# ACT and DVE take turns in copying the 1x1 units; the third depthwise unit goes between the V transposes and the mix

## The reference

```
xn   = gn(x)
qkv  = depthwise3x3(einsum('bchw,oc->bohw', xn, w_qkv) + b_qkv) + b_dw
q, k, v in windows of 8x8, 4 heads of 16 channels      # (n, head, c, 64)
attn = softmax(einsum('nhcx,nhdx->nhcd', q, k) * temperature)
out  = einsum('nhcd,nhdx->nhcx', attn, v) * gelu(einsum('nhcx,yx->nhcy', v, w_mlp) + b_mlp)
y    = x + einsum('bchw,oc->bohw', out, w_proj) + b_proj
```

## Time and profile before

| what | us |
|---|---|
| median of 3 runs | 829.38 |
| the runs | 822.47, 829.38, 843.41 |
| profiled execution, whole | 837.38 |
| its span, first to last instruction | 835.5 |
| PE matmul busy in the span | 721.4 |
| DVE busy | 512.1 |
| ACT busy | 493.9 |

### The profile page before, as it was taken

The page is one execution under the profiler, slowest core; times in us unless marked ns, Lnnn a source line. Parts: engine busy times, 40 slices in busy tenths (PEclk is TensorE's granted clock), DMA queues, the critical chain, the costliest instruction groups (busy, mean ns, idle before and its releaser), DMA issues.

```text
span 835.5 us, 40617 instructions
## 1 busy us (share of the span) xinstructions
PE 721.4 (86%) x19080; PEld 633.8 (76%) x19080; DVE 512.1 (61%) x957; ACT 493.9 (59%) x628; POOL 0.3 (0%) x5
## 2 busy tenths in 40 slices
PE   3968988988788988988979898999899898999875
PEld 3956877887676877877867877888788777788854
DVE  2714466758666665756665574767666666656554
ACT  2553455747556465756657485767566675747564
POOL 0000000000000000000000000000000000000000
PEclk9999999999999989999999999999999999999987
DMA  9723131423416031131414140121304040412022
GB/s 224 264 100 108 18 109 54 155 84 113 149 29 210 4 131 33 58 102 30 145 18 159 18 149 15 66 98 53 110 15 150 4 159 4 157 18 104 5 65 40
DMA packets 26501, 73.69 MB, mean 88 GB/s; under 512 B 9463, under 2 KB 15991, under 8 KB 21271
## 3 DMA queue, kind: packets, MB, share of 16 engines
q1 hardware_dynamic: 26076, 69.31, 26.1%
q10 hardware_dynamic: 258, 1.79, 1.2%
HBM read 54.31 MB, written 16.78 MB: 85 GB/s over the span
## 4 chain that ended last, share of the span: by engine, by line
PE 81%; DVE 8%; issue 5%; ACT 4%; DMA 1%; DVEq 0%; ACTq 0%
PE work L596 24%; PE work L576 23%; PE pair_ps L645 9%; PE score_ps L681 9%; PE pair_ps L669 5%; PE work L547 5%; PE pair_ps L654 3%; DVE z L343 3%; DVE patches L407 3%; PE score_ps L632 3%; ACT v_t L297 2%; DMA z<-in_hot 1%; DVE stats L415 1%; DVE staged L476 0%; DVE mixed L424 0%
## 5 line engine op out<-in xcount | busy, mean ns | idle before, releaser
L576 PE MATMUL work<-consts,patches 64*100 64x192 f32 x2048 | 209.6, 345 | 27.7 <-DVE patches L407 22.7
L596 PE MATMUL work<-z,dw 109*64 109x64 f32 x6144 | 202.2, 227 | 23.9 <-issue 12.4
L596 PEld LDWEIGHTS work<-z,dw 109*64 109x64 f32 x6144 | 192.6, 142 | 29.6 <-issue 26.7
L576 PEld LDWEIGHTS work<-consts,patches 64*100 64x100 f32 x2048 | 165.0, 170 | 46.5 <-issue 33.8
L275 ACT ACTIVATE z<-work 100x768 f32<-100x768 f32 x158 | 122.2, 807 | 65.4 <-PE work L576 65.2
L275 ACT ACTIVATE qkv<-work 128x1024 f32<-128x1024 f32 x63 | 64.5, 1023 | 135.5 <-PE work L596 135.5
L343 DVE COPY z<-work 100x768 f32<-100x768 f32 x98 | 90.9, 953 | 56.4 <-PE work L576 56.3
L447 DVE TENSOR_TENSOR gate<-pair_ps,consts 128x512 f32<-128x512 f32 x64 | 44.3, 692 | 92.8 <-PE pair_ps L645 92.8
L297 ACT ACTIVATE v_t<-pair_ps 128x512 f32<-128x512 f32 x64 | 38.2, 597 | 97.9 <-PE pair_ps L654 97.9
L645 PE MATMUL pair_ps<-consts,qkv 64*64 64x64 f32 x2048 | 82.3, 233 | 11.4 <-issue 7.9
L645 PEld LDWEIGHTS pair_ps<-consts,qkv 64*64 64x64 f32 x2048 | 72.1, 145 | 23.8 <-issue 14.5
(11 more groups left out here) (45 smaller groups left out, 523.4 us busy)
## 6 DMA issues: line engine op xcount, KB each, us to landing
staged<-in_x SPq DMA_DIRECT2D x18, 1024.0 KB, 4.9
out_y<-staged SPq DMA_DIRECT2D x15, 1024.0 KB, 4.5
T<-in_x SPq DMA_DIRECT2D x12, 1152.0 KB, 9.0
seen<-in_x SPq DMA_DIRECT2D x16, 512.0 KB, 4.1
qkv<-in_x SPq DMA_DIRECT2D x6, 1024.0 KB, 25.4
T<-in_x SPq DMA_DIRECT2D x3, 1088.0 KB, 9.3
z<-in_edges SPq DMA_DIRECT2D x5, 288.0 KB
out_y<-staged SPq DMA_DIRECT2D x4, 256.0 KB, 4.0
```

Source lines behind the costliest of these rows:

```text
L576: last = nc.tensor.matmul(to[0:NPATCH, t, b * QKV:(b + 1) * QKV], patches[image, b, g], w1[image], start=True, stop=True)
L596: last = nc.tensor.matmul(to[h * HW:(h + 1) * HW, m // 8, m % 8 * NW:(m % 8 + 1) * NW], dw[0:K, c, :], z[0:K, c, :], start=True, stop=True)
```

## The change

- Quarters 0 and 1: ACT copied units 0 to 4 of a step, DVE 5, 6 and 7. Now ACT copies 0, 2, 4, 6 and 7 and DVE 1, 3 and 5. ACT's copies of 6 and 7 stand behind gelu(i). DVE's copy of 1 stands between scores_up and gate_up, that of 3 between divide and turn.
- Quarters 2 and 3: PE's third depthwise unit, which stood ahead of project, now stands between turn_v and apply_probs. DVE's copy of it moves behind residual(i - 1).
- normalise(n + 1) moves from quarter 3 to quarter 2 on DVE, and what finishes the statistics of the second pair comes one step earlier on all three engines.

```diff
--- before.py
+++ after.py
@@ -61,9 +61,9 @@
         fill = [("mix", n, g) for g in range(8 * a, 8 * a + 8)]
     else:
         fill = [("dw", n, v) for v in range(3 * (a - 2), 3 * (a - 2) + 3)]
+    if (n, a) == (BANDS - 1, 0):
+        fill += [("mean", 1)]
     if (n, a) == (BANDS - 1, 1):
-        fill += [("mean", 1)]
-    if (n, a) == (BANDS - 1, 2):
         fill += [("var", 1)]
     return fill
 
@@ -319,21 +319,22 @@
                 more = n < CHUNKS
                 if more and a < 2:
                     evacuate_mix(act, copy, n, 8 * a)
-                    evacuate_mix(act, copy, n, 8 * a + 1)
                 if more and a >= 2:
                     evacuate_dw(act, copy, n, 3 * a - 6)
                 exponent(i)
                 if more and a < 2:
                     evacuate_mix(act, copy, n, 8 * a + 2)
-                    evacuate_mix(act, copy, n, 8 * a + 3)
                 if more and a >= 2:
                     evacuate_dw(act, copy, n, 3 * a - 5)
                 v_up(i)
                 if more and a < 2:
                     evacuate_mix(act, copy, n, 8 * a + 4)
-                if (n, a) == (BANDS - 1, 3):
+                if (n, a) == (BANDS - 1, 2):
                     deviation(1)
                 gelu(i)
+                if more and a < 2:
+                    evacuate_mix(act, copy, n, 8 * a + 6)
+                    evacuate_mix(act, copy, n, 8 * a + 7)
 
         @block.vector
         def _(dve):
@@ -505,29 +506,32 @@
                 n, a = i // BATCHES + 1, i % BATCHES
                 if i:
                     mix(i - 1)
+                if (n, a) == (BANDS - 1, 1):
+                    centre(1)
                 if (n, a) == (BANDS - 1, 2):
-                    centre(1)
-                if (n, a) == (BANDS - 1, 3):
                     variance(1)
                 scores_up(i)
+                if n < CHUNKS and a < 2:
+                    evacuate_mix(dve, copy, n, 8 * a + 1)
                 gate_up(i)
                 divide(i)
+                if n < CHUNKS and a < 2:
+                    evacuate_mix(dve, copy, n, 8 * a + 3)
                 turn(i)
+                if i:
+                    residual(i - 1)
                 if n < CHUNKS and a >= 2:
                     evacuate_dw(dve, copy, n, 3 * a - 4)
-                if i:
-                    residual(i - 1)
                 if i < 2 * BANDS:
                     look(i)
                 if i == 2 * BANDS:
                     aggregate(1)
-                if (n, a) == (BANDS - 1, 3):
+                if (n, a) == (BANDS - 1, 2):
                     normaliser(1)
-                if a == 3 and n + 1 < CHUNKS:
+                if a == 2 and n + 1 < CHUNKS:
                     normalise(n + 1)
                 if n < CHUNKS and a < 2:
-                    for g in range(8 * a + 5, 8 * a + 8):
-                        evacuate_mix(dve, copy, n, g)
+                    evacuate_mix(dve, copy, n, 8 * a + 5)
             mix(STEPS - 1)
             residual(STEPS - 1)
 
@@ -696,7 +700,7 @@
                 depthwise(0, v)
             for i in range(STEPS):
                 units_now = fillers(i)
-                cut = (2, 4, 6) if i % BATCHES < 2 else (1, 3, 3)
+                cut = (2, 4, 6) if i % BATCHES < 2 else (1, 2, 3)
                 if i % BATCHES == 0:
                     qkv_of(i // BATCHES)
                 score(i)
```

## The result

The changed kernel takes 846.55 us (median of 4 runs, 841.85 to 853.08), the kernel before 829.89 (4 runs, 822.47 to 843.41). The ratio is 1.0237, with a 95% interval of 1.0129 to 1.0345: slower by 1.3 to 3.5%. The forecast was slower too, but 888 us with a range from 856; it had 59 us more where 17 were measured.

The account below looks back on a forecast made before the run. PE was taken as the bound, with 81% of the chain of waits. Waits +44, issue -7 and clock +22 made +59 us on the median 829.4: 888 us, forecast 873 to 905, wider range 856 to 912.

Parts of the forecast that it names:

- Removed, 47.2 us: PE waits taken away: v_t 20.6, patches 16.2, depthwise unit 0 10.0, mean unit 0.4; 51 us with overlap.
- (a): Unit 0 of quarter 1 waits for ACT's copy of unit 6: 1.7 us, 15 chunks, 25 us (M: unit 4's start).
- (b): Depthwise unit 0 waits for ACT's copies of units 6 and 7 of quarter 1: 2.5 us, 15 times, 38 us.
- (e): The "mean" unit waits for unit 6's late copy and runs ahead of the score: about 1 us, once.
- (c): The score that opens a chunk waits for DVE's copy of the last depthwise unit: 0.8 us, 15 times, 12 us.
- (d): Gates of quarter 3 wait for mix(i), behind DVE's depthwise copy and normalise: 0.86 to 2.2 us a chunk, 19 us.
- Net of the waits, +44: All new PE waits, 95 us, less the 51 us of waits removed.
- Issue, -7: PE idle time waiting for nothing shown; a third of some 10 us per-chunk overlap with new waits saved: -7, bounds 0 and -20.
- Clock, +22: Slow PE rows after idle times, at 9 in 13: 11 us removed, 26 and 7 added; bounds -11 and +55.
- only the waits, and much of the issue time vanishes in them: Rival: clock neutral, issue -14, so 829 + 30 = 859 us; chance 0.28.
- Every new wait is followed by a slow clock: Rival: slow PE rows behind all new waits, 44 - 7 + 55 = +92, 921 us; chance 0.13.
- ACT is in time: Rival: (a) and (b) vanish, about 806 us; needs unit 6 out 1.7 us sooner; chance 0.06 with anything similar.

Follow-up runs that it names:

- Turns only: Kernel before with ACT copying units 0, 2, 4, 6, 7 and DVE 1, 3, 5, nothing else: 865.29 us, ratio 1.0468.
- longer chain: Changed kernel plus a one-element Sqrt with its table load on ACT between Gelu and the Exp, 1.48 us a step: 930.76 us, ratio 1.1263.
- Exp reload last: Changed kernel with ACT's second table load and its one-element Exp behind the copies of units 6 and 7: 804.58 us, ratio 0.9725; again 803.8 us.

## Why the prediction was wrong

The direction and the cause were right, and so were the places of the waits. Three costs were put too high: the waits for ACT by about 10 us, the waits for mixed by 13, the clock by 8 to 23, according to the profile of the kernel before. The saving of issue time was put 2 to 7 us too low. In the order of its steps, by the ledger (changed against before; idle figures):

- *Removed, 47.2 us.* v_t -20.1, patches -16.2, the mean unit 0.4 and DVE z at depthwise unit 0 10.0: 46.7. Right.
- *(a) 1.7 us ahead of unit 0, (b) 2.5 ahead of depthwise unit 0, (e) 1: 64 us.* Measured 1.47 and 2.34 as idle time in the steady chunks, with the 0.07 of overlap 1.54 and 2.41; 54.5 in all. The chain was read rightly (M + 0.94, M + 5.20); each link was 0.05 to 0.1 shorter than its duration, since a copy starts before the Exp ahead of it has ended. At the change of pairs the waits stand ahead of mean and var instead, not beside them. And in the first four chunks, those with looks, (a) is 1.07 to 1.43, because PE had already been held a little by DVE's copies at units 4 to 7 (the first pair takes 1.83 us there, the second 1.66, where 1.55 is usual). 10 us too much, or 7 where the 0.07 is counted for each of the 30 waits.
- *(c) 0.8 ahead of a chunk's first score, 12 us.* Measured 0.66 (0.59 once): 9.8. Right.
- *(d) gates of quarter 3, 19 us.* Measured 5.5, and 6.9 in the second profile (the last chunk's waits of 2.0 and 1.5 taken off). **This step failed.** The mechanism is there, in order and place, in this stretch of the changed kernel, all engines:

```profile
606.25 1.22 DVE L344 COPY qkv<-work 128x1024 f32<-128x1024 f32 x1 [1.65 <-PE work L600]
607.39 2.13 DVE L408 TENSOR_SCALAR patches<-T,norm 128x1600 f32<-128x1600 f32 x2
609.43 0.68 DVE L425 TENSOR_TENSOR mixed<-pair_ps,gate 128x512 f32<-128x512 f32 x1
...
610.17 1.21 PE L649 MATMUL pair_ps<-consts,qkv 64*64 64x64 f32 x32 [0.55 <-DVE mixed L425]
```

  The three DVE instructions take 3.86 us from the first start to the last end (606.25 to 610.11), not 1.23 + 2.12 + 0.69 = 4.04, and 0.55 is what is left. More than that: of the 14 chunks only seven show the wait at all. In all the others an issue stall of 0.45 to 1.3 us stands in the score or the depthwise unit just ahead of these gates and has used it up. The four chunks with looks and the change of pairs, put at 2.2 each, show 0.37 to 1.26, and there too a stall of 0.62 to 1.11 stands just ahead; stall and wait together are 1.5 to 1.9. Only two of the 14 chunks, with waits of 0.55 and 0.88, have no stall there. The second profile has its waits in the same seven chunks (0.55 to 1.43) and its stalls in the same twelve. I had put such absorption in a term of its own for all places together and had not seen that this place is where stalls of the kernel before already were: both of its profiles have one in this stretch in the same 8 of 15 chunks.
- *Net of the waits, +44.* Measured 54.5 + 9.8 + 5.5 - 46.7 = +23. Half of it.
- *Issue, -7.* Measured from 28.0 or 30.7 to 19.4 or 16.9: -9 to -14. The bound of -20 held. "Turns only" and the longer chain agree (13.5 and 14.9), and every kernel without the long ACT waits keeps 28 to 36. So a long wait behind score takes in the stalls, more than I gave it; what the stalls are, no run here shows.
- *Clock, +22.* Measured by PE's busy time: -1 against the profile I worked from, +11 to +14 against the second one. **This step failed too.** Taken row by row (what each row takes over its usual duration, up to the next idle time), the slow rows behind the 30 waits for ACT z hold 17.6 us in one profile and 17.7 in the other, and 12 of the 30 waits have them; the sum had 33. The rate "9 of 13 idle times of 1.4 us and more" was carried over to the new waits, at a third even to those of 1.47 us; these were followed by a slow row in none of 28 cases. The 11 us that I took off as removed are 5 in the second profile of the same kernel, at the same waits for patches: half of them belonged to the execution. That error made the forecast too low, so it hid part of the miss.
- *Sum.* for the first pair of profiles +23 - 9 - 1 = +13, and the spans differ by 10; of the 3 us between, 1.1 is a shorter wait ahead of the first matmul, and the rest is not accounted for; against the second profile of the kernel before +23 - 11 + 11 = +23, and the spans differ by 22. The medians of the runs say +17.

Of the rivals, "only the waits, and much of the issue time vanishes in them", 859 us, was the nearest, and it too had the 44. "Every new wait is followed by a slow clock" is not so here (12 of 30); with waits 1.5 us longer it holds ahead of the depthwise unit (14 of 14) and not ahead of unit 0 (8 of 14). "ACT is in time" named the right lever, one of the two table loads: with it moved, the time is 804.6, and the rival's figure was 806. That they agree so closely is partly luck: 11.6 us of waits for ACT z are left there, and gates pays 8.6 in all where the rival had 19 of new waits.

Of what was to be seen in the changed profile, the waits for v_t, patches and qkv came as written, those for ACT z in place but shorter, and those for mixed, named as 0.9 to 2.2, were 0.37 to 1.26; the granted clock was 0.967, not lower than 0.963. The sign of being wrong that the prediction named for the copy did not come: ACT's copy of unit 6 begins 582.70 - 577.59 = 5.11 us after unit 4. That sign tested the cause, which was right, and not the sizes.

## What to carry to other kernels

Cost a moved copy from the earliest time at which its engine can begin it, with everything that is queued ahead, table loads too: here two copies behind a Gelu and an Exp reload turned a gain of 2% into a loss of 2%, and moving the reload behind them brought the gain back. When a sum has several new waits in one loop, look at each whether the stalls of the old profile already stand there, since the same microsecond is not lost twice. The two profiles of the kernel before agree on where these stalls are, so the place can be looked up. Slow-clock time is less steady: take a second profile of the kernel before, if one can be had, before any of it is booked as something that the change will remove.

## What the runs showed of the hardware

- The cost of a PE wait is not one to one, and its length alone does not say what it costs. Ahead of unit 0, behind single idle times of 1.07 to 1.47 us, the row was never slow (28 of 28 at 1.60), and behind 2.6 to 3.0 us in 8 of 14. Ahead of depthwise unit 0, behind 1.5 to 2.5 us, the unit, usually 2.08, took 2.6 to 3.7 in 21 of 28, and behind 3.6 to 3.9 us it took 3.4 to 3.8, always. So waits of 1.5 to 2.5 us at the second place are followed by slow rows more often than longer ones at the first; why is not shown. Short waits are no safeguard either: in the kernel with the depthwise move alone, where 1.3 to 2.5 us follow a wait of 0.66 at once, 8 of 14 were slow. Lengthening 30 waits by 1.48 us cost 47 us of idle time and 35 us of PE's busy time.
- The Trainium skill says on the page "TensorE: Matmul & The Clock Gate" (A second HAM failure mode) that PE idling briefly between matmul groups makes the clock swing. These runs agree for the waits of 1.5 us and more ahead of the depthwise unit (21 of 28); for the single waits up to 1.47 ahead of unit 0 they show nothing of it.
- Issue stalls stand at fixed places of the program: 27 of 29 at the same matmul in two profiles of the kernel before, 21 of 23 in the two of the changed kernel. Their lengths change from one execution to the next, and a long wait shortly behind can take them in.
- An ACT copy out of PSUM needs no table load behind either table: in "Exp reload last" it starts before Gelu's end (517.52, Gelu until 517.62), in the changed kernel before the Exp's.
